# One attention head in four: its row maximum as b + relu(a - b), with ScalarE taking the relu

## The reference, cut to what matters

```python
scores = jnp.einsum('bhsk,bhtk->bhst', Q[..., :KPH], K) / math.sqrt(KPH)
attn = jax.nn.softmax(scores, axis=-1)
ao = jnp.einsum('bhst,bhtv->bhsv', attn, V)
```

## Time and profile before

| | |
|---|---|
| timed runs | median 4025.93 us (4025.74 to 4030.18) |
| span of the profiled execution | 4055.7 us (the profile gives no other time of it) |
| granted TensorE clock, mean over the span | 0.920 |
| attention stage | about 1887 to 3310 us of the span |
| busy over the span | PE 84%, DVE 79%, ACT 59%, POOL 32% |

### The profile page before, as it was taken

The page is one execution under the profiler, slowest core; times in us unless marked ns, Lnnn a source line. Parts: engine busy times, 40 slices in busy tenths (PEclk is TensorE's granted clock), DMA queues, the critical chain, the costliest instruction groups (busy, mean ns, idle before and its releaser), DMA issues. The chain is left out here.

```text
span 4055.7 us, 64760 instructions
## 1 busy us (share of the span) xinstructions
PE 3421.6 (84%) x19475; PEld 2015.0 (50%) x19476; DVE 3205.1 (79%) x4243; ACT 2410.3 (59%) x4320; POOL 1304.2 (32%) x905
## 2 busy tenths in 40 slices
PE   8968989987559799897999999999999964389950
PEld 3445555554448689795333333333333322189950
DVE  8959999998876466467899999999999923378768
ACT  6768888885964433210577777777777750133323
POOL 4439989986014444301000000000000006644520
PEclk9979999998889899997799999999999986699975
DMA  6664444444859733395122323232232124223258
GB/s 213 251 210 168 162 157 160 163 158 148 278 180 251 201 89 92 91 291 143 26 53 61 68 55 73 53 72 57 57 71 52 31 70 126 83 81 91 89 168 294
DMA packets 531451, 521.08 MB, mean 128 GB/s; under 512 B 84784, under 2 KB 441264, under 8 KB 531040
## 3 DMA queue, kind: packets, MB, share of 16 engines
q1 hardware_dynamic: 517248, 480.45, 40.3%
q0 software_dynamic: 13952, 37.74, 2.7%
HBM read 301.15 MB, written 215.71 MB: 127 GB/s over the span
## 5 line engine op out<-in xcount | busy, mean ns | idle before, releaser
L2315 DVE TENSOR_REDUCE at_top<-at_psM 128x1 f32<-128x1024 f32 x1024 | 1205.6, 1219 | 101.2 <-PE at_psM L2174 99.8
L2283 ACT ACTIVATE at_probs<-at_psS 128x512 f32<-128x512 f32 x2048 | 1061.0, 603 | 286.3 <-PE at_psS L2200 286.3
L2200 PE MATMUL at_psS<-at_q,at_k 64*128 64x512 f32 x2048 | 803.6, 471 | 8.2 <-ACT at_probs L2283 8.2
L2174 PE MATMUL at_psM<-at_k,at_q 62*128 62x512 f32 x2048 | 705.2, 454 | 41.4 <-DMA at_vraw<-scratch_vf 21.9
L575 POOL TENSOR_TENSOR sc_prod<-sc_state,sc_c_row 128x1024 f32<-128x1024 f32 x256 | 648.7, 2564 | 84.7 <-DVE sc_state L726 72.6
L2174 PEld LDWEIGHTS at_psM<-at_k,at_q 62*128 62x128 f32 x2048 | 312.9, 190 | 621.6 <-DVE at_top L2315 539.6
L726 DVE TENSOR_TENSOR_SCAN sc_state<-sc_dec,sc_psI 128x1024 f32<-128x1024 f32 x256 | 574.3, 2276 | 43.7 <-PE sc_psI L647 34.0
L2213 PE MATMUL at_psV<-at_probs,at_v 128*32 128x512 f32 x4096 | 546.3, 605 | 0.0
L658 PE MATMUL sc_psY<-sc_prod,sc_ident 128*128 128x512 f32 x1024 | 480.4, 599 | 15.3 <-DVE sc_y L712 15.3
L2200 PEld LDWEIGHTS at_psS<-at_q,at_k 64*128 64x128 f32 x2048 | 337.7, 184 | 170.3 <-ACT at_probs L2283 160.5
L2141 POOL COPY at_v<-at_vraw 128x256 f32<-128x256 f32 x32 | 12.8, 401 | 1250.4 <-DMA at_vraw<-scratch_vf 1167.5
(11 more groups left out here) (398 smaller groups left out, 4928.7 us busy)
## 6 DMA issues: line engine op xcount, KB each, us to landing
sc_c_row<-scratch_bc SPq DMA_DIRECT2D x128, 512.0 KB, 3.7
scratch_xs<-at_zeros SPq DMA_DIRECT2D x140, 264.0 KB, 4.7
sc_b_row<-scratch_bc SPq DMA_DIRECT2D x32, 512.0 KB, 5.0
ec_y<-scratch_ys SPq DMA_DIRECT2D x32, 512.0 KB, 6.1
ex_x<-scratch_xs SPq DMA_DIRECT2D x39, 264.0 KB, 2.8
si_x<-in_x SPq DMA_DIRECT2D x16, 512.0 KB, 4.4
scratch_xn<-si_xn SPq DMA_DIRECT2D x16, 512.0 KB, 5.1
scratch_x_t<-si_xT SPq DMA_DIRECT2D x16, 512.0 KB, 5.7
```

The source lines that it names most:

```text
L2174: ins = pe.matmul(psM[t % 2][:, half * TILE:(half + 1) * TILE], rows_of(q4[j], h, 0, MAXROW)[:, c * P:(c + 1) * P], rows_of(k4[j], h, 0, M ...
L2200: pe.matmul(psS[v % 3][:], rows_of(k4[j], h, 0, GROUP)[:, c * P:(c + 1) * P], rows_of(q4[j], h, 0, GROUP)[:, half * TILE:(half + 1) * TILE ...
L2283: act.activation(probs[:, slot(j, v), :], psS[v % 3][:], ACT.Exp).then_inc(act_done, 1)
L2315: dve.tensor_reduce(top[j % 2][:, h, c:c + 1], psM[t % 2][:], AX.X, ALU.max, negate=True).then_inc(maxed, 1)
```

## The change

One tile of four (t % 4 = 3, which is head 2) gets its maximum in another way. With a its scores against the first 512 keys and b those against the last 512:

- `negative_keys` (GpSimd): `kn[j]` = minus the last 512 keys of head 2, once a unit.
- `difference` (TensorE): two matmuls accumulate a - b into a `psS` buffer. It takes an entry of its own in the three-buffer ring that scores and exponentials go through. It stands behind the two steps in which t % 4 = 1, two steps ahead of its tile, and so behind S4 and ahead of V in every second cycle.
- `raised` (ScalarE): relu(a - b) into `mag`, in the order of the ring, between S4's exponential and the next S1's.
- `maxima` of that tile computes b alone (one matmul of 512 columns, not two).
- `maximum` of that tile on VectorE: one TENSOR_TENSOR_REDUCE over 512 columns, -(b + relu(a - b)) and its minimum, in place of the reduction of 1024 columns.

The zeroing of `k4` and `q4` is shared: groups 0 and 1 by VectorE, 2 and 3 by GpSimd, with the ones made after it and sent behind all four loads. `cleared.make` moves behind GpSimd's first copies of the values. The loops of SyncE and GpSimd are unrolled.

```diff
+    DIFF = 3
+    DIFF_HEAD = HEADS[DIFF]
+    score_at, diff_at, turn_at, entries = {}, {}, {}, 0
+    for v, t in [(0, t) for t in range(MT)] + [(1, t) for t in range(LEAD)]:
+        if t % QUAD == 1:
+            diff_at[v, t + 2], entries = entries, entries + 1
+    turn_at[0], entries = entries, entries + 1
+    for u in range(UNITS):
+        for s in range(MT):
+            for n in (2 * s, 2 * s + 1):
+                score_at[u, n], entries = entries, entries + 1
+                if n == TURN and u + 1 < UNITS:
+                    turn_at[u + 1], entries = entries, entries + 1
+            v, t = u + 1 + (s + LEAD) // MT, (s + LEAD) % MT
+            if v < UNITS and t % QUAD == 1:
+                diff_at[v, t + 2], entries = entries, entries + 1
...
+        kn = [m.sb(f"kn{j}", [MAXROW, TILE], F32R) for j in range(NQ)]
+        mag = [m.sb(f"mag{k}", [P, TILE]) for k in range(2)]
...
             @block.sync
                 for j in range(NQ):
-                    sp.wait_ge(ready_made, 2 * j + 3)
+                    sp.wait_ge(zeroed[j], 2)
                     m.settle(sp)
                     load(0, j)
+                sp.wait_ge(ones_made, 1)
+                m.settle(sp)
+                for j in range(NQ):
                     for group in range(2):
                         dst = k4[j][GROUP * group + MAXROW:GROUP * (group + 1), :, :].bitcast(F32)
                         sp.dma_start(dst, ones[:]).then_inc(ones_in, 16)
...
             @block.gpsimd
-                cleared.make(pool)
+                for j in range(2, NQ):
+                    pool.memset(k4[j][:].bitcast(F32), 0.0).then_inc(zeroed[j], 1)
+                    pool.memset(q4[j][:].bitcast(F32), 0.0).then_inc(zeroed[j], 1)
...
+                def negative_keys(b, j):
+                    pool.wait_ge(loaded[j], (b + 1) * 16 * LOADS)
+                    pool.tensor_scalar(kn[j][:], rows_of(k4[j], DIFF_HEAD, 0, MAXROW)[:, TILE:T].bitcast(F32), -1.0, None,
+                                       ALU.mult).then_inc(kn_ready[j], 1)
...
+                negative_keys(0, 0)
                 for j in range(NQ):
                     pool.memset(v4[j][:], 0.0).then_inc(v_ready, 1)
...
+                for b in range(1, B):
                     for j in range(NQ):
+                        negative_keys(b, j)
                         spread_values(b, j)
...
             @block.tensor
+                def maxima(u, t, half):
+                    j, (h, c) = u % NQ, tile_of(t)
+                    if t % QUAD == DIFF and half == 0:
+                        return
+                    if half == (1 if t % QUAD == DIFF else 0) and u * MT + t > 1:
+                        pe.wait_ge(maxed, u * MT + t - 1)
+                    at = 0 if t % QUAD == DIFF else half
...
+                def free(e):
+                    if e >= 3:
+                        pe.wait_ge(act_done, e - 2)
+                def difference(u, t):
+                    j, (h, c), e = u % NQ, tile_of(t), diff_at[u, t]
+                    free(e)
+                    pe.wait_ge(kn_ready[j], u // NQ + 1)
+                    query = rows_of(q4[j], h, 0, MAXROW)[:, c * P:(c + 1) * P]
+                    pe.matmul(psS[e % 3][:], query, rows_of(k4[j], h, 0, MAXROW)[:, 0:TILE], start=True, stop=False)
+                    pe.matmul(psS[e % 3][:], query, kn[j][:], start=False, stop=True).then_inc(keyed, 1)
...
+                def step(u, s):
+                    v, t = u + 1 + (s + LEAD) // MT, (s + LEAD) % MT
+                    more = v < UNITS
...
                     for half in range(NHALF):
                         if more:
+                            maxima(v, t, half)
                         n = 2 * s + half
+                        scores(u, n)
+                        if n == TURN and u + 1 < UNITS:
+                            turn(u + 1)
+                    if more and t % QUAD == 1:
+                        difference(v, t + 2)
...
             @block.scalar
+                def raised(u, t):
+                    e, k = diff_at[u, t], t // QUAD % 2
+                    act.wait_ge(keyed, e + 1)
+                    if u * MT + t >= 2 * QUAD:
+                        act.wait_ge(maxed, u * MT + t + 1 - 2 * QUAD)
+                    act.activation(mag[k][:], psS[e % 3][:], ACT.Relu).then_inc(act_done, 1)
...
             @block.vector
-                for j in range(NQ):
-                    dve.memset(k4[j][:].bitcast(F32), 0.0).then_inc(ready_made, 1)
-                    dve.memset(q4[j][:].bitcast(F32), 0.0).then_inc(ready_made, 1)
+                for j in range(2):
+                    dve.memset(k4[j][:].bitcast(F32), 0.0).then_inc(zeroed[j], 1)
+                    dve.memset(q4[j][:].bitcast(F32), 0.0).then_inc(zeroed[j], 1)
...
+                def maximum(u, t):
+                    h, c = HEADS[t % QUAD], t // QUAD
+                    at = top[u % 2][:, h, c:c + 1]
+                    if t % QUAD != DIFF:
+                        dve.wait_ge(scored, u * MT + (t + 1))
+                        dve.tensor_reduce(at, psM[t % 2][:], AX.X, ALU.max, negate=True).then_inc(maxed, 1)
+                        return
+                    dve.wait_ge(act_done, diff_at[u, t] + 1)
                     dve.wait_ge(scored, u * MT + (t + 1))
+                    raised = mag[t // QUAD % 2]
+                    dve.tensor_tensor_reduce(raised[:], psM[t % 2][:, 0:TILE], raised[:], -1.0, 3e38, ALU.add, ALU.min,
+                                             at).then_inc(maxed, 1)
```

More of the change, by code:

```diff
@@ L2164, in tile_of @@
                     return HEADS[t % QUAD], t // QUAD
[L2166 to L2174, removed]
+                def maxima(u, t, half):
[5 more added lines that the diff above has]
+                    at = 0 if t % QUAD == DIFF else half
+                    ins = pe.matmul(psM[t % 2][:, at * TILE:(at + 1) * TILE],
                                     rows_of(q4[j], h, 0, MAXROW)[:, c * P:(c + 1) * P],
@@ L2197, in scores, with turn @@
+                def turn(u):
+                    e = turn_at[u]
+                    free(e)
+                    top_at.wait(pe, u, "rest")
+                    pe.transpose(psS[e % 3][:, 0:P], top2[:], ident[:]).then_inc(keyed, 1)
+                def scores(u, n):
+                    j, e = u % NQ, score_at[u, n]
                     half, c, h = n // (KC * QUAD), n // QUAD % KC, KEYED[n % QUAD]
-                    v = at_slot[n]
-                    free(u, v)
-                    pe.matmul(psS[v % 3][:], rows_of(k4[j], h, 0, GROUP)[:, c * P:(c + 1) * P],
+                    free(e)
+                    pe.matmul(psS[e % 3][:], rows_of(k4[j], h, 0, GROUP)[:, c * P:(c + 1) * P],
@@ L2212, in values @@
                     for n, h in enumerate(KEYED):
-                        last = pe.matmul(psV[32 * h:32 * h + 32, :], v4[j][:, c, h, :], probs[:, slot(j, at_slot[4 * g + n]), :],
+                        last = pe.matmul(psV[32 * h:32 * h + 32, :], v4[j][:, c, h, :], probs[:, slot(u, 4 * g + n), :],
                                          start=(c == 0), stop=(c == KC - 1))
                     last.then_inc(summed, 1)
[L2217 to L2222, removed]
+                def step(u, s):
+                    v, t = u + 1 + (s + LEAD) // MT, (s + LEAD) % MT
+                    more = v < UNITS
@@ L2223, in step @@
                     if more and t == 0:
-                        pe.wait_ge(loaded[mj], mb * 16 * LOADS + 16 * LOADS)
+                        pe.wait_ge(loaded[v % NQ], (v // NQ + 1) * 16 * LOADS)
                     for half in range(NHALF):
                         if more:
-                            maxima(u + ahead, mj, t, half)
+                            maxima(v, t, half)
                         n = 2 * s + half
-                        scores(u, j, n)
-                        if n == TURN:
-                            turn(u, not last_unit)
@@ new lines, in step @@
+                        if n == TURN and u + 1 < UNITS:
+                            turn(u + 1)
+                    if more and t % QUAD == 1:
+                        difference(v, t + 2)
+                for u, count in ((0, MT), (1, LEAD)):
+                    pe.wait_ge(loaded[u], 16 * LOADS)
+                    for t in range(count):
+                        for half in range(NHALF):
+                            maxima(u, t, half)
+                        if t % QUAD == 1:
+                            difference(u, t + 2)
@@ new lines, in _ @@
+                for u, count in ((0, MT), (1, LEAD)):
+                    for t in range(DIFF, count, QUAD):
+                        raised(u, t)
+                turned(0)
+                for u in range(UNITS):
+                    for s in range(MT):
+                        for n in (2 * s, 2 * s + 1):
+                            exponential(u, n)
+                            if n == TURN and u + 1 < UNITS:
+                                turned(u + 1)
```

(3 more changed lines are left out.)

178 lines of the change are left out of this document (65 added, 113 removed).

## The result

The changed kernel takes 4194.7 us (4193.55 to 4196.15), the kernel before beside it 4028.05 us: a ratio of 1.0417, with a 95% interval of 1.0405 to 1.043. It is slower by 167 us.

The account below looks back on a forecast made before the run. The prediction took a 2.62 us loop of scores, exponential and value matmuls, without VectorE, as the bound. The difference's +175 us and the prologue's -6 gave +169: 4025.9 + 169 = 4195 us, eight-in-ten range 4150 to 4250.

Parts of the forecast that it names:

- The loop that it found: TensorE and ScalarE, steady cycle: first score, its exponential, fourth score, value matmuls, next first score; 2.62 us, no VectorE instruction.
- D's price: TensorE, every second steady cycle: the difference's two matmuls between fourth score and value matmuls cost 0.71 us.
- the steady part: Steady attention cycles: 246 differences at 0.71 us each add 175 us, bounds 59 and 226.
- the prologue: Before the steady cycles: shared zeroing starts the first reduction 5.9 us earlier; -6 us taken, between -14 and +2.
- What bounds the kernel: Steady attention stage: VectorE, though busy 185.62 of 200 us, does not set the pace; its 0.49 us saved gains nothing.
- ScalarE's relu free: ScalarE, steady cycles: 256 relus of 0.60 us fit idle time and cost nothing beyond the difference's delay.
- VectorE's new operation: VectorE, one tile of four: two-input operation over 512 columns takes 0.69 us, bounds 0.60 and 1.35.
- GpSimd's pass over the keys: GpSimd, once a unit over 62 x 512: costs nothing, at most under 1 us in the first unit.
- the rival of a faster kernel: Steady part: VectorE sets the pace, its relief gains 120 us, 126 with the prologue; 3900 us; chance 0.05.

Follow-up runs that it names:

- V shorter: Kernel before with exponentials and values in bfloat16, which shortens the value matmuls: 3921.5 us, ratio 0.9734.
- the small relu: Changed kernel with the relu over 8 of 512 columns, the difference's two matmuls kept: 4194.1 us.
- a short V and D off the ring: Changed kernel with the difference's matmuls in the free half of their tile's psM buffer, exponentials and values in bfloat16: 3866.0 us, ratio 0.9596 to the kernel before in float32.
- the three kernels in bfloat16: Exponentials and values in bfloat16 in the kernel before (3921.5 us), the changed kernel (3926.9) and the changed kernel with the difference off the ring (3866.0).

## Why the prediction was right

The loop that it found sets the pace, and D's price in it came out as summed. That the time itself was met within 1 us is partly luck: the steady part was 2 us under its term, and the prologue gained 1 us less than its own.

- What bounds the kernel: right, and shown from both sides: half of VectorE's reductions away, no change in the unit; V shorter, 105 us less at once (3933 forecast, 3921.5 measured).
- D's price: 0.71 forecast, (47.73 - 42.04) / 8 = 0.71 measured. Each piece was where it was put: D 0.49 behind S4, its second matmul 0.33 later, V 0.33 after that. The two runs that move or halve D split the price: 0.49 for the entry of the ring, at either place, and 0.22 for the second matmul behind the wait. The weight load of the second matmul starts 0.10 into the first (2569.70 against 2569.60). The Trainium skill (TensorE: Matmul & The Clock Gate, "The mechanism") says that a load overlaps with matmuls in flight only when its row group differs; that does not hold here either. The same section of the Trainium skill also has loads pulled ahead when they go to a background weight buffer, and these rows would fit that.
- The steady part: from the first score to the last it was 3306.7 - 1961.0 = 1345.7 us and is 3472.2 - 1953.1 = 1519.1: +173, forecast +175. The scores of before and of after (ns min/median/max, first and last start):

```profile
L2200 PE MATMUL at_psS<-at_q,at_k x2048: 383/493/792, 1961.0 to 3306.7; 64*128 64x512 f32 x187
```
```profile
L2230 PE MATMUL at_psS<-at_q,at_k x2048: 386/492/792, 1953.1 to 3472.2; 64*128 64x512 f32 x187
```

- The prologue: the first reduction stands 1899.50 - 1884.70 = 14.8 us behind the stage's first memset, and stood 19.6; 4.8 us, forecast 5.9. Half of the 1.1 us that are missing is the first two matmuls: the forecast took 0.8 us for them, and the reduction started 1.3 behind TensorE (1899.50 - 1898.20), at a granted clock of 0.50 (mean from 1900 to 1955 us). The loads, 9.0 us from issue to TensorE's start and not 8.4, are the other half. From there to the first score next to nothing changed (53.6 against 54.1), as forecast. The memsets of the two engines did not get in each other's way: 1.81 and 1.76 us side by side in the timeline after, which also has the first reduction and the pass over the keys.

```profile
1884.70 1.81 POOL L2140 MEMSET at_k<- 128x2048 f32 x1 [4.14 <-POOLq L3153]
1885.20 1.76 DVE L2330 MEMSET at_k<- 128x2048 f32 x1 [6.13 <-PEq L3153]
...
1889.20 0.36 SPq L2090 DMA_DIRECT2D at_q<-scratch_qs  x1
...
1898.15 1.52 POOL L2150 TENSOR_SCALAR at_kn<-at_k 62x512 fp32r<-62x512 f32 x1 [5.83 <-DMA at_vraw<-scratch_vf]
...
1898.20 1.23 PE L2199 MATMUL at_psM<-at_k,at_q 62*128 62x512 f32 x4 [20.45 <-DMA at_vraw<-scratch_vf]
...
1899.50 2.36 DVE L2340 TENSOR_REDUCE at_top<-at_psM 128x1 f32<-128x1024 f32 x2 [3.85 <-PE at_psM L2199]
...
1899.72 0.28 PEld L2215 LDWEIGHTS at_psS<-at_k,at_q 62*128 62x128 f32 x1 [1.02 <-POOL at_kn L2150]
```

The Trainium skill (SBUF — State Buffer, "SBUF: two separate sides") has the shared port pair taken by a VectorE instruction in a 2-port mode or with two inputs in SBUF. A memset has no input, and nothing here puts one in such a mode, so the prediction gave this rule more weight against the sharing than it has. No memset here shows it.

- ScalarE's relu free: right, the small relu shows it. No loads of tables between Exp and Relu.
- VectorE's new operation: 0.68 and 0.08 for reading out its accumulator, forecast 0.69; it had no bearing. It never stood idle for the relu (0.0 before L2346), as forecast.
- GpSimd's pass over the keys was under-sized: 1.5 us, forecast under 1. It held up the very first difference by about 1 us (1.02 in the last row above) and nothing after.
- The span of the profiled executions differs by 137 us, the medians by 167. From the last score to the end the profiled execution of before took 749 us, that of the change 721; no step of the change lies there, and the medians don't show it. The ten other profiles have 714 to 719 us there, so that the odd one is the profile of before. So the difference of two single spans would have misled; the sum over the terms did not.
- The other side: the rival of a faster kernel had 120 us for VectorE's relief. It was wrong for this kernel. With a short V and D off the ring, the relief was worth 55 us, about half of that.

## What to carry to other kernels

A list that charges 500 us of waits to one engine doesn't make it the bound; look for a stretch that lacks its work altogether (here the last 20 cycles) and compare the period. Where a ring of few buffers and one engine's order close a loop, an extra entry makes the last wait one exponential longer (0.49 us here, at both of the places that were tried); its work behind that wait comes on top (0.22), and its work put into the wait costs nothing more. Only off the ring, in the time of the wait, was the same work free. Work moved off an engine pays only when the loop is shorter than that engine, so shorten the loop first, and then look at the granted clock too: here it fell in the kernel whose short V left TensorE idle for 9 of 38 us.

## What the runs showed of the hardware that I had not expected

- GpSimd takes 1.48 to 1.52 us to negate 62 x 512 elements of float32 into fp32r, against 0.39 for its copy of 128 x 256.
- The four matmuls of V, side by side on columns of the array, are recorded as eight in float32, and the next score stands 1.00 us behind their start. In bfloat16 they are recorded as four, and the next score stands most often 0.33 us behind their start in the change, 0.47 in the kernel before. One V of the changed kernel in bfloat16:

```profile
2504.56 0.40 PE L2243 MATMUL at_psV<-at_probs,at_v 128*32 128x512 bf16 x4
...
2504.89 0.49 PE L2230 MATMUL at_psS<-at_q,at_k 64*128 64x512 f32 x1
```

- With a short V TensorE's granted clock falls to 0.50 now and then, and for most of the last 20 cycles; those took 52 to 54 us in the three kernels in bfloat16, against 51 in float32 at 1.00.
